# Another hand-written order for the five engines, and other PSUM banks, in a two-layer Macaron block

## What is computed

```python
x = x + 0.5 * _L0_ffn_ref(_layernorm(x), ...)   # gate, up 256 -> 704, silu(gate) * up, down; int weights
x = x + _L0_attn_ref(_layernorm(x), ...)        # 16 heads of 16, rope, causal softmax
x = x + 0.5 * _L0_ffn_ref(_layernorm(x), ...)
x = x + 0.5 * _L1_ffn_ref(_layernorm(x), ...)   # weights rounded to -1, 0, 1; sigmoid(gate) * up
x = x + _L1_attn_ref(_layernorm(x), ...)        # 16 query heads, 4 key heads, alibi bias, causal
x = x + 0.5 * _L1_ffn_ref(_layernorm(x), ...)
```

## Time and profile before

| | us |
|---|---|
| runs | 586.17, 580.11, 585.03 |
| median | 585.03 |
| the profiled execution | 586.17 |
| its span, first to last instruction | 584.2 |

### The profile page before, as it was taken

How to read it: one execution, slowest core, us unless ns; L and a number is a source line. 1 busy time by engine, 2 the same in 40 slices (tenths; PEclk the granted TensorE clock), 3 DMA queues, 4 the chain that set the end, 5 groups by cost and what they waited for, 6 DMA issues and landing times.

```text
span 584.2 us, 12653 instructions
## 1 busy us (share of the span) xinstructions
PE 535.6 (92%) x4924; PEld 290.7 (50%) x4924; DVE 461.8 (79%) x813; ACT 401.5 (69%) x605; POOL 340.4 (58%) x427
## 2 busy tenths in 40 slices
PE   2887987998999999999899998999999999999987
PEld 1353642544653654655546564465455644553664
DVE  4888979898889789589986878887897767783454
ACT  5866576678577758855687756867769596669433
POOL 2367886864896578844645167624455724437543
PEclk9978997999999999999999999999999999999999
DMA  8700020121022100310210102010211021001301
GB/s 327 311 2 1 22 88 1 55 74 42 20 85 65 37 4 3 121 65 1 77 40 3 47 17 74 22 41 0 69 41 38 4 78 50 22 1 41 111 0 73
DMA packets 19627, 31.73 MB, mean 54 GB/s; under 512 B 6464, under 2 KB 7872, under 8 KB 19416
## 3 DMA queue, kind: packets, MB, share of 16 engines
q1 hardware_dynamic: 19568, 30.93, 15.0%
HBM read 13.75 MB, written 2.36 MB: 28 GB/s over the span
## 4 chain that ended last, share of the span: by engine, by line
PE 57%; DVE 14%; ACT 9%; POOL 7%; issue 7%; DMA 5%; SPq 1%; DVEq 0%; POOLq 0%; ACTq 0%
PE PS L583 17%; PE PS L607 10%; PE PS L694 9%; PE PS L674 4%; DVE MX L1050 4%; PE PS L625 4%; PE PS L659 4%; PE PS L567 3%; ACT PB L838 3%; PE PS L709 3%; DMA RB<-scratch 2%; ACT XN L761 2%; PE PS L539 1%; DVE MX L1046 1%; DVE ST L863 1%
## 5 line engine op out<-in xcount | busy, mean ns | idle before, releaser
L838 ACT ACTIVATE PB<-PS 128x1024 f32<-128x1024 f32 x160 | 158.9, 1024 | 50.3 <-PE PS L674 43.2
L1050 DVE TENSOR_REDUCE MX<-PS 128x2 f16<-128x1024 f32 (+2 forms) x192 | 158.4, 865 | 23.1 <-PE PS L539 22.9
L583 PE MATMUL PS<-XT,WGU 128*128 128x512 f16 x660 | 158.2, 382 | 2.8 <-DVE PB L990 1.1
L1126 POOL TENSOR_TENSOR HH<-TH,HH 128x512 f16<-128x512 f32 x71 | 82.2, 1168 | 86.1 <-ACT HH L806 85.8
L1154 POOL TENSOR_SCALAR_AFFINE_SELECT PB<-PB 128x512 f32<-128x512 f32 (+1 forms) x140 | 73.2, 550 | 53.1 <-ACT PB L838 53.1
L583 PEld LDWEIGHTS PS<-XT,WGU 128*128 128x128 f16 x660 | 59.1, 98 | 74.1 <-issue 5.9
L607 PE MATMUL PS<-WD,HH 128*128 128x256 f16 x660 | 78.0, 273 | 1.1 <-POOL HH L1126 0.6
L694 PE MATMUL PS<-PB,V 128*32 128x512 f32 (+3 forms) x1024 | 75.5, 435 | 1.3 <-POOL PB L1154 1.1
L607 PEld LDWEIGHTS PS<-WD,HH 128*128 128x128 f16 x660 | 62.4, 98 | 14.0 <-issue 3.1
L659 PE MATMUL PS<-SK,SQ 63*128 63x256 f16 (+3 forms) x512 | 60.7, 300 | 6.5 <-DVE MX L1050 3.6
L674 PE MATMUL PS<-SQ,SK 64*128 64x384 f16 (+3 forms) x512 | 58.5, 300 | 8.0 <-ACT PB L838 2.4
(11 more groups left out here) (122 smaller groups left out, 756.4 us busy)
## 6 DMA issues: line engine op xcount, KB each, us to landing
SQ<-QPB SPq DMA_DIRECT2D x24, 256.0 KB, 2.5
OC<-OT SPq DMA_DIRECT2D x16, 256.0 KB, 2.4
RB<-scratch SPq DMA_DIRECT2D x32, 128.0 KB
SK<-QPB SPq DMA_DIRECT2D x12, 256.0 KB, 3.1
SQ<-MT SPq DMA_DIRECT2D x128, 1.0 KB
out<-X SPq DMA_DIRECT2D x8, 256.0 KB, 2.2
PB<-gu SPq DMA_DIRECT2D x2, 704.0 KB, 6.1
X<-x_in SPq DMA_DIRECT2D x2, 512.0 KB, 5.4
```

The source lines that it names most:

```text
L583: m = e.matmul(o[:, :], WGU[l][:, k, col:col + P], rows_of(f)[j][:, k, :], start=j == 0 and k == 0, stop=j == 1 and k == 1)
L838: e.activation(PB[Q % 2][:, j, :, :], two_banks("s", i), ACT.Exp, scale=0.25).then_inc(a_exp, 1)
L1050: e.tensor_reduce(mx[:, :, pr, t], o[:, :, col:col + (t + 1) * P], AX.X, ALU.max, negate=True).then_inc(a_max, 1)
L1126: e.tensor_tensor(hh[1][:, s * T:(s + 1) * T], value_of(j)[0], hh[0][:, s * T:(s + 1) * T], ALU.subtract).then_inc(f_lo, 1)
```

## The change

Only the strings in `ORDER` change. Each keeps its letters and their counts, so that every item, its instructions and its waits on data are as before; the order on each engine changes, and with the banks the items whose read TensorE awaits. Out of place are 205 of 714 items of TensorE (by at most 5 places), 185 of 530 of VectorE, 239 of 533 of ScalarE (at most 9), 145 of 295 of GpSimd, 33 of 106 of SyncE. 159 of 666 PSUM items get another bank. The core of the diff, first line of each string:

```diff
 ORDER = {
     "sp":
-        "kkrrkrkrDSrRDSRrkrDSRkrrDSRrrDrkSRkDSRrrlkkrDrSRrDSlRrkrkDrSRrDSrRrkkrDrSRDrSRrDkrkSRDrSRrrrDSRDOSOR"
+        "kkrrkrkDrSrRDSRrrDkSkRrrDSrRrDrSRkkDSRrrkkrlrDSRrDSRlrkkrDrSRrDSrRrkkrDrSRDSRrrDkrkSRDrSRrrOrODSRDSR"
         "OOOOOO",
     "pe":
-        "ttggGggGaGgttGGggGggddddGaGgtggGuutGqqddddvqgGgvgqGGGgugugGqttqmmgmgmmmmmqmsqsdsmgGmsdmsdmmsdsmmpmsG"
...
+        "ttgggGgGgaGgttGGgGgdddagdtgGGtggGuuGqqddvddgqGvggqGGGgugugGqttqmmmgmgmmmmqmsqsdsmGgmsdmsdmsmdsmmpmss"
...
     "dve":
-        "NwNtthwwhwkhwhwhtwthwwNhhwwdwNdwhnhwhkuuhtpqptqdwdpqhnpqhhkuuhhhpqttqpmmmmmxmmmspqsmhpmqxhmdmsmmdmxm"
...
+        "NwNtthwwhwhwkwhwthtwwhwNhhwdwNdwhnhwhkuuhtqptqpdwdpqnhhpqhkhuuhhqpttpqmmmmmxmmmpsqmphsmqxhmdmsmmdmkx"
...
     "act":
-        "TwwXxxwttthXtthxxhhwhtwhkttwwwthwhXtkhwxthYwyyhthXxkQQvtkthQtvYQtyytthhxxhhQTkQkktthkeeeteeQeeQhhoee"
...
+        "TwwXxxwttthwXwtthxhxhwhtwhtwkkthwXtwtxhhtxYhwyythhQXktvQvkthtQhYQtytythhkxxkQQhhTtketekeeteeQehQoeee"
...
     "pool":
-        "wrwwrhhhhwhwrdhdrewhhhhsasqdadsqaesaqqhwshsahahqqhfsafsdfafqdhqfffffhefhffcfhCffhcCssaaqqfffrssadaqq"
...
+        "wrrwwhhhwhhwrddhhewhrhhsasdqadsqaesaqqhwsaqsaqhhhhsfsafdfadfqqffefhhffhhfffcCfffhcCsasafqqffrssaadqq"
...
 
     "banks":
-        "7657247041575464537217560127506743163251703463712537543705126021464265264656210622642062605264062506"
...
+        "1613427054610524135413226554653063613623704641201276542437624602164265264656201622642602605260425620"
...
 }
```

More of the change, by code:

```diff
@@ new lines @@
+        "GsgmmsGsspmsgsmmGmmpsmssmgssGmmmpsmsvsvmsmsuummmpqsqoooosdsdsmsqmqpsmttdmsdssmgggsgGGpmmgsmGsmssmmgs"
+        "GGmmmpmssvvmsuudsdmddsqmsqoopmottosmsgsqsmggmgGGsGgmspsmmgGssGqttpsssdgssdddgGgpgGgmvmmmvgmGuGmuGmoo"
+        "oomqmsqmssqdmsmddmmsdmssmmspsmssmmmsttspsgsmgmgGgGgsmGGGgsmpssmtddtddssmggmpmvmgGguusGGsqgsmqsmgGsqs"
+        "mGoosmpmmddddmsmsompomsmtstssggGssGsgmmpsgmGmsgmsmGgGmpsmvsmsmsmmdddsmdsspsmttsmogmsgouugGooqqqGsmms"
+        "gmsGGgGgmspmmsmdmsdsmsddsmspsmmssmmspttvmsmgggGgGGGggGsmmssttssddddoooommmpspuusmmqgqsqsgsgGsGsspssm"
@@ new lines @@
+        "gmmmGpmgvmmgGmGmsmsmsststmmpdddmsdoosmogsosmmsgGgGmsmpmgsssGsgsgsspssGGttpddddggGggGGggGGoooodddttdg"
+        "ggGgGGgGgGdddd",
+    "dve":
+        "NwNtthwwhwhwkwhwthtwwhwNhhwdwNdwhnhwhkuuhtqptqpdwdpqnhhpqhkhuuhhqpttpqmmmmmxmmmpsqmphsmqxhmdmsmmdmkx"
+        "mmnhmshmmxmsmhmmcmmsxmmmmcxhmmumumpqmpqooNmxdqpqpmmtcmtdmxshnskhsshmmmmhmmsxshmmhmmcxumudmdNpmoqqmpt"
+        "tomxNhmmhpqhkmhmmxhcqhpttsdhdksnhsshcmsmmmmhsumuxhmohommllmxlmmdmmdmxmNmmmmmttxNmhckhhmmhhhmxmtdtdnm"
+        "mssmhcmksuuhshhxmlmsslhmhmlmmdoxdmNmmmoxmttNhchmmkhmhmmxhmhmmmcxmmmdmdnmttxmmsohusukhollslhmmsmhshms"
+        "xhmmmmcxdmdmNmmmmNttcxmhmhkhhhhmmdxttdnommomNuumlmxhlclhhkmmmmhmxmmhmmmhcmxmmtdmdtomxhomNkmhmmhmxhch"
+        "htctddhhkhhhhooNXtthdkhhhdhhdd",
@@ new lines @@
+    "act":
+        "TwwXxxwttthwXwtthxhxhwhtwhtwkkthwXtwtxhhtxYhwyythhQXktvQvkthtQhYQtytythhkxxkQQhhTtketekeeteeQehQoeee"
+        "theeheoeteYhhoeeeteeoeevecveeyhyceoQeQeeeXoexQxeQeteethtthoeheetetheYoeehvhcvyeyeeceXoxxQeeeetthtXhe"
+        "QhettoheQeethxhxoeeeetQehttcothtvhYtyvcyhhQheQeeQeeeeeoeeXexxeeoeetthtthhetXhthheexoexeettoYchtvyyet"
+        "ehQehthetQcehQeheoeeXoexxeeteteeehhtoehtetehhtXhoeveeeceeecoexxeYtetyhytQhQQeethethtehhoeeeeeeoeeeXe"
+        "coxxevtXthththhttheheexxeceYoeoyyeQXtQeQeetteeehoeethhothtvcheeeeehxocexeteeethtXehohteeeeheeteteehh"
+        "xxootthhcttchthhthXxxthttthhhthth",
@@ L139 @@
+        "rbfhfhfhchhbCcCefffhhfhhhfdffdfrfcrChhhhhcCfbfefrffffffhchhChhcCffrfhfhffhbfffhhchcCChhhhrhhhhh",
     "banks":
[L140 to L143 removed]
@@ L144 @@
[L144 to L146 removed]
+        "1613427054610524135413226554653063613623704641201276542437624602164265264656201622642602605260425620"
+        "4065024620562406420562406250265070264012640126714046241652065216464207240167205624062062461026416205"
@@ new lines @@
+        "7426106472462105643562056460326350612460462106430216204762027062745240625407216356246204364023460640"
+        "2420620506204624672147026053273462045620246124306431606402635407205402602752460526036413604230240624"
+        "3624750260420725042056024714704264026047024247206740264075142017260426142604764212642064264162406240"
+        "6206450162403270574156024603264060162406304620756240526027025206526045621640365026026056402615267046"
+        "702406263720462046412642043047612703275130671235262103453157160265",
```

26 lines of the change are left out of this document (1 added, 25 removed).

## The result

| | before | changed |
|---|---|---|
| median of 10 runs, us | 584.69 | 587.76 |
| lowest and highest | 580.11, 586.17 | 584.89, 589.87 |
| ratio, with its 95% interval | | 1.0076 [1.0056, 1.0096] |
| the profiled execution | 586.17 | 588.59 |
| its span | 584.2 | 586.9 |

The change makes the kernel slower by 0.76% (0.56 to 0.96), which is 4.4 us. The ratio is taken over more executions than the ten shown; their medians alone differ by 3.1 us. The record lists 43 of the changed kernel, with a median of 588.62 us. By the bound of the prediction, 1%, that is no change, and the time lies in the range given; but it is told apart from before, and on the other side of it than forecast. The profiled run of before is the longest of the ten, so the two profiles differ by 2.4 us only, 588.59 - 586.17.

What follows compares the result with a forecast made beforehand. Bound: TensorE from 100 to 560 us, VectorE, GpSimd and ScalarE work before. Terms -1.1 + 0.15 + 0.2 + 0 + 0, then -0.75 for the clock, gave -1.5: 584.7 us, or 583.6 on the median's scale; range 577 to 591.

Steps and rivals of the forecast that it cites:

- Setup, first half: 16 to 54 us: idle times of VectorE before N3 and d0 go, -1.1 us; bounds -2.0 and +4.2.
- the disputed size: VectorE's w5, started while GpSimd still waits, could give back between 0 and 0.9 of its 2.25 us; not counted.
- Setup, second half: 54 to 100 us: VectorE through 0.65 us sooner, p6 +0.5, GpSimd's r3 and h6 +0.3; sum +0.15, bounds -1.5 and +2.
- SyncE, +0.2: Transfers at 280 to 291 us: s70's 0.70 us wait goes, late l0 costs m80 +0.9; bounds -0.7 and +2.0.
- The steady part: TensorE's waits from new banks and places: -1.8 + 2.1 = +0.3 us, taken as 0; bounds -3.5 and +3.5.
- The end: From 566.28 us: TensorE still runs 9.66 and 4.97 us of matmuls without a pause, 0; bounds -0.5 and +0.7.
- The clock, -0.75: First stretch at half clock, in the early part: gain of -0.75 us, between 0 and -2.9.
- The clock that stays up: Early part: two of three stretches at half clock vanish, 5.9 us less, 578.4 us; chance 0.22.
- ScalarE's early conversions: w3 and w4 ahead of t3 and t4, 19 to 25 us, become the path: +7.1, 592.2 us; chance 0.17.
- The third: Whole kernel: every freed wait reappears at the next one, 585.0 us; chance 0.25.
- my signs: Marks of a right forecast, among them TensorE idle 16 to 20 us from 100 to 560 us, three half-clock stretches.
- e90: Steady part: the forecast's name for the item that o14's new bank waits for, a wait of +0.6 us.

Runs made afterwards that it cites:

- the changed start alone: The changed order until about 102 us on every engine, the order of the kernel before from there on: 584.43 us, ratio 0.9994.
- The windows behind 346 us: The kernel before with the changed order only at 346 to 370, 370 to 392, 392 to 410 us, or from 410 us on: 1.0020, 1.0015, 1.0015, 1.0016.

## Why the prediction was wrong

- **Setup, first half, -1.1.** The mechanism is there. TensorE's g6, GpSimd's WO subtraction and VectorE's N3 are the three rows below. The subtraction starts at 35.29 us (near 36 predicted, 38.11 before); d0 and N3 no longer wait; VectorE's idle time from 16 to 60 us is 4.31 us, 4.42 before; and g6, in bank 1 behind g5, waits for ScalarE's t5 as foreseen, though until 30.45 us only and not 32.1:

```profile
30.45 4.45 PE L583 MATMUL PS<-PB,WGU 128*128 128x512 f16 x12 [2.60 <-ACT TH L794]
...
35.29 1.15 POOL L1090 TENSOR_TENSOR WO<-RB,WO 128x512 f16<-128x512 f32 x1
...
38.71 1.39 DVE L863 BATCH_NORM_STATS2 ST<-X 128x6 f32<-128x256 f32 x4
```

  N3 even starts 2.5 us earlier than at 41.24. One reason is the disputed size: the second half of w5 on VectorE (L937) took 1284 ns where it took 2250, so 0.97 us came back. Its row before and changed:

```profile
L937 DVE SCALAR_TENSOR_TENSOR WD<-OC,GS,SQ x1: 2250/2250/2250, 23.9 to 23.9; 128x1024 f16<-128x1024 f32 x1
```

```profile
L937 DVE SCALAR_TENSOR_TENSOR WD<-OC,GS,SQ x1: 1284/1284/1284, 24.0 to 24.0; 128x1024 f16<-128x1024 f32 x1
```

  That is the larger of the two values I had weighed, the one that follows if a VectorE instruction with two SBUF inputs and a GpSimd instruction reading SBUF exclude each other (the Trainium skill, SBUF — State Buffer, "Who interferes with whom"); the change started it while GpSimd was still waiting for its first h. Yet 2.5 us on VectorE at 41 us are 1.9 us on TensorE at 54 us, and the changed start alone is worth 0.35 us [-0.6, 1.3] at the end. The term of -1.1 is inside that interval, and nothing shows that it reached the end in full.
- **Setup, second half, +0.15.** u3 follows without a wait (0.83 before), as predicted. By TensorE's delay the stretch from t5 to q7 is -0.4 us, inside the bounds; the profiles differ in half clock too there, so I can't size it better.
- **SyncE, +0.2.** In mechanism right, in size too small. r14 left at 283.28 us, not 287.20, and l0 from 285.56, a little earlier than the 286.7 that I had, m80 was ready at 288.9 and waited 1.37 us, below my mark of 1.5; s70 waited 0.29 us, for an exponential, and not 0.70 for the transfer. The two waits together went from 0.70 to 1.66 us, +0.96 and not +0.2, inside my bounds. In the changed order the part until 346 us is at 1.0006, and its interval, up to 1.0026, leaves room for this. What I had not seen is that the price of the same move was 1.8 us in the kernel before and nothing in the changed one, since it depends on whether VectorE has maxima in hand.
- **The steady part, 0.** This is the step that failed. I had named 1.8 us of waits that go and 2.1 that come, among them the right ones: o14's bank at +0.6 (measured +0.85) and s153 at +0.5 (measured +1.0). I then took 0 for the sum and not even its +0.3. The windows behind 346 us measure 1.2, 0.9, 0.9 and 0.9, together 3.9 us, where my bound was 3.5; by their intervals this sum is uncertain by some 2 us. Behind it stands a premise, that an exchange of two ready items costs zero "because the same instructions fill the same time". It doesn't hold: m103 between g57 and G47 costs 0.21 us without any wait. Three more things were missed: the waits of scores for VectorE's maxima, which went from 0.9 to 2.7 us from 281 to 560 us (2.5 to 3.4 over all lines), and which I had not looked for; s93's bank, 0.89 us; and that t20's and t18's freed waits would be taken by the next item (t20 freed 0.46 us, and s109 waits 0.35 for maxima a little later), while new waits weren't absorbed in the same way. The 18.3 us of idle time that I read as the most that could be won says nothing about what could be lost.
- **The end, 0.** Right: 9.66 and 4.97 us again without a pause, now from 568.99 us.
- **The clock, -0.75.** The sum calls 0.75 a third of 2.9 us, and it is a quarter. The first stretch was indeed shorter, but it is so in kernels with the old start too, so the change earned nothing. I had worked from one execution, whose clock was not the usual one, and had noted only that it was the longest of three.
- **Rivals.** The clock that stays up (578.4) didn't come. ScalarE's early conversions (592.2) didn't become the path: VectorE's idle time did not grow. The third, that nothing reaches the end, fits the first 346 us within the interval and fails behind it. The loss came from a side that I had no rival for: many small waits in the steady part, in the one place where I had written "0, bounds 3.5".
- **Signs and readings.** Of my signs, idle TensorE from 100 to 560 us came out at 20.9 us, outside the 16 to 20, and there are four stretches at half clock and not three. In the clock row only slices 3, 4 and 7 are below 9, not 3 to 7 and the last. The exponential that o14 waits for is that of s89, which I called e90.

What stays open: how the 1.0 us from 392 to 410 us and the 0.8 behind it divide among single items, and how much of them is banks and how much places.

## What to carry to other kernels

Where an engine is the bound at 96%, a new order of ready items is not free on both sides: a freed wait can be taken by the next item, as with t18 and t20, while a buffer given to an item that comes one or two places behind its last user makes a wait that nothing ahead can hide. Two ready items of different kinds don't change places for nothing either: an exchange that splits a run of like matmuls cost 0.21 us here. Check for each reassigned bank how many items lie between its last reader and its new user. And price a late transfer by the engine that is next to the limit there: the same move cost 1.8 us in one order and nothing in another. When a large exchange of orders gives little, cut it where both orders have done the same items, look in the profile for seams of one's own cut before believing a window's time, and compare the time that the same items take in all profiles, which tells 0.2 us where the medians of 12 runs don't tell 0.9.
